# Queries and keys made once for all heads, scores for two heads together, and three smaller edits in a four-stage megakernel

## The reference, cut to what matters

```python
x = x + 0.5 * ffn0(layernorm(x))      # gate and up to 352, silu, down; inputs and weights rounded to FP4 by blocks of 16
x = x + mamba(layernorm(x))           # 2 layers: 256 channels, 16 states, scan over 256 steps, softplus for the step size
x = x + 0.5 * ffn0(layernorm(x))
x = x + 0.5 * moe(layernorm(x))       # 8 experts, 128 -> 512 -> 128; weight p where p > 0.5, p = sigmoid(x @ Wg + bg)
x = x + attention(layernorm(x))       # 16 heads of 8, causal, relative bias; LayerNorm with gain and shift inside
x = x + 0.5 * moe(layernorm(x))
# attention: q = proj(Wq) / sqrt(8); k = proj(Wk); v = proj(Wv)
#            softmax(q @ k.T + bias[distance], causal) @ v, then @ Wo.T
# rounding:  scale = max(|block|) / 6; q = nearest of 0, .5, 1, 1.5, 2, 3, 4, 6 of |x / scale|, times sign and scale
```

## Time and profile before

| | |
|---|---|
| median of 3 runs | 2702.1 us |
| the profiled execution | 2699.89 us |
| its span, first to last instruction | 2698.1 us |
| PE busy | 2506.0 us, 93% |
| DVE busy | 1943.5 us, 72% |
| ACT busy | 1612.1 us, 60% |
| POOL busy | 1367.7 us, 51% |
| mean granted TensorE clock | 0.969 |
| DMA | 56 GB/s on the mean |

### The profile page before, as it was taken

How to read it: one execution, slowest core, us unless ns; L and a number is a source line. 1 busy time by engine, 2 the same in 40 slices (tenths; PEclk the granted TensorE clock), 3 DMA queues, 4 the chain that set the end, 5 groups by cost and what they waited for, 6 DMA issues and landing times.

```text
span 2698.1 us, 41593 instructions
## 1 busy us (share of the span) xinstructions
PE 2506.0 (93%) x14781; PEld 1756.5 (65%) x14781; DVE 1943.5 (72%) x3913; ACT 1612.1 (60%) x3465; POOL 1367.7 (51%) x1227
## 2 busy tenths in 40 slices
PE   7999999997898999887899999998999999999988
PEld 7888885785565655655555765756556656566665
DVE  5878798789787788687787688788787868532420
ACT  1424436443886567653776558664976786466754
POOL 1466474847373656456363745557373738321111
PEclk9999999998998999998999999998999999999989
DMA  4123121312121113112120212122120213000000
GB/s 153 52 75 102 46 90 48 94 56 71 42 85 32 56 47 96 45 58 63 47 80 33 78 41 63 48 67 63 40 87 29 79 41 94 17 5 1 1 5 5
DMA packets 88573, 150.59 MB, mean 56 GB/s; under 512 B 10565, under 2 KB 21485, under 8 KB 88110
## 3 DMA queue, kind: packets, MB, share of 16 engines
q1 hardware_dynamic: 88366, 147.94, 17.8%
HBM read 145.26 MB, written 2.65 MB: 55 GB/s over the span
## 4 chain that ended last, share of the span: by engine, by line
PE 75%; ACT 10%; DVE 8%; issue 4%; POOL 3%; DMA 0%; POOLq 0%; SPq 0%; DVEq 0%; ACTq 0%
PE c_bank L1369 16%; PE c_bank L924 15%; PE c_bank L916 14%; PE a_bank L762 7%; PE a_bank L752 3%; PE b_bank L1083 2%; DVE hst L710 2%; PE b_bank L1072 2%; PE a_bank L731 2%; PE b_bank L584 2%; ACT weighted_y L959 1%; DVE a_bank L704 1%; PE b_bank L565 1%; PE a_bank L768 1%; PE a_bank L736 1%
## 5 line engine op out<-in xcount | busy, mean ns | idle before, releaser
L833 POOL TENSOR_TENSOR prod_c<-hst,prod_c 128x512 f32<-128x512 f32 x512 | 666.3, 1307 | 411.1 <-DVE hst L710 384.0
L710 DVE TENSOR_TENSOR_SCAN hst<-dA,a_bank 128x512 f32<-128x512 f32 x512 | 621.8, 1214 | 14.8 <-ACT dA L822 4.5
L822 ACT ACTIVATE dA<-delta,a_neg 128x510 f32<-128x510 f32 x512 | 364.7, 719 | 320.5 <-DVE hst L710 314.8
L916 PE MATMUL c_bank<-c_xT,w 128*128 128x512 f32 x1024 | 532.4, 624 | 23.5 <-ACT weighted_y L959 11.8
L924 PEld LDWEIGHTS c_bank<-w,hid 128*128 128x128 f32 x4096 | 487.5, 192 | 57.9 <-ACT hid L951 26.8
L1369 PEld LDWEIGHTS c_bank<-ident 128*128 128x128 f32 x4004 | 484.6, 193 | 47.8 <-issue 39.3
L924 PE MATMUL c_bank<-w,hid 128*128 128x128 f32 x4096 | 511.1, 277 | 1.6 <-ACT hid L951 1.5
L1369 PE MATMUL c_bank<-ident 128*128 128x128 f32 x4004 | 491.8, 277 | 0.3 <-ACT weighted_y L959 0.3
L951 ACT ACTIVATE hid<-c_bank,b 128x512 f32<-128x512 f32 x512 | 349.1, 687 | 150.0 <-PE c_bank L916 147.4
L975 POOL TENSOR_TENSOR xs<-xs,weighted_y 128x512 f32<-128x512 f32 x128 | 167.5, 1309 | 497.3 <-ACT weighted_y L959 496.2
L704 DVE TENSOR_TENSOR a_bank<-du,a_bank 128x512 f32<-128x512 f32 x512 | 349.8, 683 | 72.6 <-PE a_bank L752 69.9
(11 more groups left out here) (182 smaller groups left out, 3159.8 us busy)
## 6 DMA issues: line engine op xcount, KB each, us to landing
prod_c<-c_rows SPq DMA_DIRECT2D x512, 256.0 KB, 3.2
w<-in_w SPq DMA_DIRECT2D x2, 2048.0 KB
xs<-in_x SPq DMA_DIRECT2D x8, 256.0 KB, 7.2
bias<-skew SPq DMA_DIRECT2D x1, 2048.0 KB, 8.4
out_dram<-xs SPq DMA_DIRECT2D x8, 256.0 KB, 2.3
in_wT<-in_in_wT SPq DMA_DIRECT2D x1, 512.0 KB
c_rows<-bcC SPq DMA_DIRECT2D x16, 32.0 KB, 1.6
b_hq<-in_w_gu SPq DMA_DIRECT2D x1, 384.0 KB, 3.3
```

What stands on the lines that cost most here:

```text
L710: nc.vector.tensor_tensor_scan(hst[:, s % RS, :], dA[:, s % RA, :], b_bank, 0.0, ALU.mult, ALU.add).then_inc(M.h.sem, 1)
L822: nc.scalar.activation(half_batches(dA[:, s % RA, :], 1), half_batches(delta[:, h, :], 1), ACT.Exp, scale=a_neg[:, l, h, n:n + 1]).then_in ...
L833: nc.gpsimd.tensor_tensor(prod[:, s % RP, :], hst[:, s % RS, :], cring[:, s % RC, :], ALU.mult).then_inc(M.pp.sem, 1)
L916: nc.tensor.matmul(S.bank[up_bank(e, c)][:, :], w1[:, e, c * 128:(c + 1) * 128], S.xT[:, :], start=True, stop=True).then_inc(M.up.sem, 1)
```

## The change

1. **q and k.** The weights are laid out once, with no copies. One k product into bank 1 and one q product into bank 0 for each group. ACT copies q once, DVE clears the lower 12 bits of q and k and subtracts (four operations for each group where there were sixteen). SP writes the two parts to DRAM, six DMAs of 256 KB into `qk_rows`, waits for them, and reads them back in eight DMAs (four strips for q, four for k) in the threefold layout. The first scores wait for these.
2. **Scores.** Two heads at a time, one into bank 0 and one into bank 1. Both transposes of the exponentials go through bank 2, which also holds the products with v; so each fourth transpose waits for DVE's division as well. The exponentials have four buffers, not three.
3. **Quantizer.** The subtraction (L509) moves from DVE to POOL, ahead of the rescaling.
4. **Softplus.** The larger of x and 0 is combined with the correction term while ACT takes the logarithm; behind the logarithm stands one addition instead of two operations.
5. **Gate and division.** The gate's factor 0.5 is folded in (one DVE operation fewer for each mixture pass), and the division by the row sums is one DVE operation, not two.
6. **Order strings.** All five are written anew; 1987 spare products instead of 2002; SP has a lane b.

```diff
 ORDER_PE = (
-    "b2d10bd53bd4b2d7b2d8b2d31bd4b3d43b5dbd61adbda3b2d10b2ad6ab2a2d7ad27ad4bd9b3ad6ad28a2d4ad8ad2ad5ad13a2d9ad14"
+    "b2d9bd48bd4b2d7b2d7b2d33bd4b3d43b5dbd58ad4a3bd4b2d2ad3b2dad3b2a2d5ad27ad6bd9b3ad6ad29a2d10ad14a2d8ad8ad8b5ab"
...
 ORDER_PE = (
...
-    "c2bcbc2bc2bc74")
+    "b2cbc2bcb2cbc2bcb2cb6d4b3d7bd4b3d8bd4bd4bd4bd4b4d28c68")
...
 ORDER_SP = (
-    "a215c2a73caca64caca73ca62ca39c3")
+    "a165b2ab2a65c2a5b2a2b2a59c2a7b2a2b2a55c2a2b2ab2a65cb2ab2a53baba3b2a8ca33b4cb4c2")
...
-        pr = att_buf[:, 768:1920].rearrange("p (b n) -> p b n", b=3)
+        pr = att_buf[:, 768:2304].rearrange("p (b n) -> p b n", b=4)
...
             if rounded is not None:
-                nc.vector.tensor_tensor(xq, xq, c, ALU.subtract).then_inc(rounded.sem, 1)
+                ins.then_inc(rounded.sem, 1)
...
+            nc.gpsimd.tensor_tensor(q[0][:, 0:n], q[0][:, 0:n], q[1][:, 0:n], ALU.subtract).then_inc(L.sem, L.one())
+            yield
+            pool.wait_ge(L.sem, L.n)
             nc.gpsimd.tensor_tensor(dst.rearrange("p (b s) -> p b s", s=BLK), q[0][:, 0:n].rearrange("p (b s) -> p b s", s=BLK),
...
+            for h in range(HALVES):
+                dve.wait_ge(L.sem, step[h])
+                nc.vector.scalar_tensor_tensor(out=delta[:, h, :], in0=S.bank[h][:, :], scalar=0.0, in1=delta[:, h, :],
+                                               op0=ALU.max, op1=ALU.subtract).then_inc(L.sem, L.one())
...
-                nc.vector.tensor_tensor(xc[:, h, :], xc[:, h, :], delta[:, h, :], ALU.subtract).then_inc(L.sem, L.one())
-                yield
-                dve.wait_ge(L.sem, L.n)
-                nc.vector.scalar_tensor_tensor(out=delta[:, h, :], in0=S.bank[h][:, :], scalar=0.0, in1=xc[:, h, :],
-                                               op0=ALU.max, op1=ALU.add).then_inc(M.delta.sem, 1)
+                nc.vector.tensor_tensor(delta[:, h, :], delta[:, h, :], xc[:, h, :], ALU.add).then_inc(M.delta.sem, 1)
...
+            dve.wait_ge(M.qE.sem, L.at(M.qE, 1))
+            nc.vector.tensor_scalar(q_hi.bitcast(I32), q_lo.bitcast(I32), TOP12, None, ALU.bitwise_and).then_inc(M.qH.sem, 1)
+            yield
+            dve.wait_ge(M.k.sem, L.at(M.k, 1))
+            nc.vector.tensor_scalar(k_hi.bitcast(I32), S.bank[1][:, :].bitcast(I32), TOP12, None, ALU.bitwise_and).then_inc(M.kH.sem, 1)
+            yield
+            dve.wait_ge(M.qH.sem, L.at(M.qH, 1))
+            nc.vector.tensor_tensor(q_lo, q_lo, q_hi, ALU.subtract).then_inc(M.qS.sem, 1)
+            yield
+            dve.wait_ge(M.kH.sem, L.at(M.kH, 1))
+            nc.vector.tensor_tensor(k_lo, S.bank[1][:, :], k_hi, ALU.subtract).then_inc(M.kS.sem, 1)
+            yield
...
-            for g in range(HG):
-                if g:
-                    pe.wait_ge(M.qE.sem, L.at(M.qE, g))
-                nc.tensor.matmul(S.bank[0][:, :], wqT[:, g, :], S.xT[:, :], start=True, stop=True).then_inc(M.q.sem, 1)
-                yield
-                if g:
-                    pe.wait_ge(M.kH.sem, L.at(M.kH, g))
-                nc.tensor.matmul(S.bank[1][:, :], wkT[:, g, :], S.xT[:, :], start=True, stop=True).then_inc(M.k.sem, 1)
-                yield
+            nc.tensor.matmul(S.bank[1][:, :], wkT[:, :], S.xT[:, :], start=True, stop=True).then_inc(M.k.sem, 1)
+            yield
+            nc.tensor.matmul(S.bank[0][:, :], wqT[:, :], S.xT[:, :], start=True, stop=True).then_inc(M.q.sem, 1)
+            yield
...
+            def scores(r, queries, keys, part):
+
+                b, h = r // HEADS, r % HEADS
+                p0, s0 = 32 * (h % 4), b * SEQ
+                return nc.tensor.matmul(S.bank[r % 2][:, part], qT[p0:p0 + 3 * DH, h // 4, s0 + queries:s0 + queries + 128],
+                                        kT[p0:p0 + 3 * DH, h // 4, s0:s0 + keys], start=True, stop=True)
...
+                        pe.wait_ge(s_qk, 16 * 8 * (L.g + 1))
+                        pe.wait_ge(M.kS.sem, L.at(M.kS, 1))
...
+                    if w:
+                        pe.wait_ge(M.m.sem, L.at(M.m, 2 * w))
+                    for r in (2 * w, 2 * w + 1):
+                        scores(r, 128, 256, slice(0, 256))
+                    scores(2 * w, 0, 128, slice(256, 384))
+                    scores(2 * w + 1, 0, 128, slice(256, 384)).then_inc(M.s.sem, 1)
+                    yield
...
+        def b_sp(sp, L):
+
+            for g in range(GROUPS):
+                L.g = g
+                rows = a["qk_rows"][g]
+                sp.wait_ge(att.qH.sem, L.at(att.qH, 1))
+                for p in (0, 1):
+                    sp.dma_start(rows[0, p], q_hi).then_inc(s_qkd, 16)
+                sp.wait_ge(att.kH.sem, L.at(att.kH, 1))
+                for p in (0, 2):
+                    sp.dma_start(rows[1, p], k_hi).then_inc(s_qkd, 16)
+                yield
+                sp.wait_ge(att.qS.sem, L.at(att.qS, 1))
+                sp.dma_start(rows[0, 2], q_lo).then_inc(s_qkd, 16)
+                sp.wait_ge(att.kS.sem, L.at(att.kS, 1))
+                sp.dma_start(rows[1, 1], k_lo).then_inc(s_qkd, 16)
+                yield
+                sp.wait_ge(s_qkd, 16 * 6 * (g + 1))
+                for i in range(2):
+                    strips = rows[i].rearrange("p (i j g) n -> (p i) j g n", i=DH, j=4)
+                    dst = qk[:, i, :, :].bitcast(F32)
+                    for j in range(4):
+                        sp.dma_start(dst[32 * j:32 * j + 3 * DH, :, :], strips[:, j, :, :]).then_inc(s_qk, 16)
+                    yield
```

336 lines of the change are left out of this document (142 added, 194 removed).

## The result

The changed kernel takes 2632.2 us (median, 2628.19 to 2634.66) against 2703.1: ratio 0.9736, interval 0.9718 to 0.9755, 2.6% faster. Timed again beside later experiments it took 2633.0 us, ratio 0.9749 (0.9731 to 0.9767), though single runs then went from 2626 to 2642. The forecast was 2618, range 2570 to 2680.

A forecast was written before the change was run, and what follows sets the result against it. The prediction took PE to bound most of the kernel. Its terms, 41.3 + 38.4 + 3.3 + 5 - 5 = 83 us, came off 2699.9 us, giving 2616.9, or 2619 beside the median; it predicted 2618 us, range 2570 to 2680.

The forecast's parts named there:

- The bound: PE, busy 93% of the span and 75% of the chain of waits, bounds most of the program.
- The sign of being wrong that I gave: PE's idle time growing much beyond 192 us while its real work falls by 80: new order or DVE's maxima bound.
- Part 1: q and k products on PE, 32 each down to 8 each: 48 x 0.86 = 41.3 us go.
- Part 2: Scores on PE in pairs of heads, 0.44 us instead of 0.74: 38.4 us gained, bounds nothing and 47.4.
- Part 3: Spare products on PE: 15 fewer, 3.3 us; 28 ahead of the last mixture, 5 us gained (bounds 0 and 6).
- Part 4: q and k through DRAM before each group's first scores: trip about 15 us, bounds 12 and 25; 5 us lost.
- rival D: Slower by SP's queue: 30 us trips give 2710 us; decides from a trip of 28 us on; chance 0.10.
- The covers: PE work ordered behind each group's q product to hide the DRAM trip: 13.0 to 24.2 us, 142 in all.
- Part 5: Other engines: DVE loses 156 us, 17 gained; POOL gets 79 more, 5 lost; the rest set off, counted zero.
- Rival C: POOL's subtraction comes onto the chain, half of 48 delaying lane a: 50 us, 2668 us; chance 0.12.
- The sum: Whole kernel: 41.3 + 38.4 + 3.3 + 5 - 5 = 83 us gained, 2618 us predicted, 3.1% faster.
- Rival B: More comes free: lighter DVE takes a fifth of PE's holes, 40 us, giving 2578 us; chance 0.12.

The follow-up runs named there:

- after: The changed kernel itself, with all parts of the change, against the kernel before: 2632.2 us, ratio 0.9736; timed again 2633.0 us, ratio 0.9749.
- x2: Changed kernel with each group's q and k product made four times over into the same bank: 2674.7 us, ratio 0.9902 to the kernel before.
- x12: Kernel before with 3 of 4 q and k products only 8 columns wide, all else kept: 2696.3 us, ratio 0.998.
- x1: Changed kernel with both heads of a pair read from one 32-partition strip instead of two: 2668.9 us, ratio 0.9879 to the kernel before.
- x7: Changed kernel without the 28 spare products before the last mixture: 2641.8 us, ratio 0.9765 to the kernel before.
- x9: Changed kernel with 18 more spare products before the last mixture pass but one: 2635.0 us, ratio 0.9752 to the kernel before.
- x3: Changed kernel without the q and k transfers through DRAM from the second group on: 2623.1 us, ratio 0.9712 to the kernel before.
- x4: Changed kernel with the quantizer's subtraction back on DVE and GpSimd's piece left empty: 2647.8 us, ratio 0.9803 to the kernel before.
- x11: Kernel before with only the quantizer's subtraction moved from DVE to GpSimd: 2713.8 us, ratio 1.0051.
- x6: Changed kernel with SP's reads of q and k right behind its writes: 2634.9 us, ratio 0.9754 to the kernel before.
- x5: Changed kernel with q and k tile rows 16 bytes apart, so reads go as 2 KB pieces: 2639.3 us, ratio 0.9771 to the kernel before.

## Why the prediction was right, and where it was not

**The bound.** Right for after, wrong in its wording: "work taken from PE shortens the time nearly one for one". x2 shows that work added costs one for one. x12 shows that 32 us taken from the kernel before, with its order and the steps of ACT and DVE between the products as they were, give 5. An order written by hand has no work waiting to fill a hole. That the change got its gain because the order was written anew around the shorter work is argued, not shown: no run has the new strings without the parts, or the parts without the strings. The sign of being wrong that I gave came half true: PE's idle time grew by 19 us while its work fell by 91. It is not DVE's two maxima, for which PE itself does not wait and its weight loads wait 3.8 us; nor has another engine replaced the bound.

**Part 1, q and k.** 41.3 us expected, 43.6 gone from PE (60.6 to 17.0), 45 when put back (x2). 16 and 16 records, as expected.

**Part 2, the pairs, is the term that was mis-sized on PE.** I took 0.44 us for a pair, since no row showed weight loads side by side; it is 0.375, the upper bound. 47.7 us left PE, not 38.4, and x1 gives 32 to 39 of time for one step between. The rule of the Trainium skill that I weighed (TensorE: Matmul & The Clock Gate, Part 3: Packing small matmuls), that matmuls in different row groups run at the same time and a weight load overlaps them, gave the right number here.

**Part 3, the spares.** The 15 fewer are 3.3 us. The last mixture's clock is 0.99 as said; x7 puts the 28 between 2.5 and 9 us, not told from nothing by the interval. What I missed is that the order lost 40 spares one mixture earlier (putting 18 back changed nothing, x9), and that the clock fell behind lane a as a whole, from 0.98 to 0.94.

**Part 4, the way through DRAM.** The step that failed is the landing of the reads. The steps ahead of them came about as counted: the writes landed 7.8 to 8.2 us after the q product's start in five of the groups, and my terms give 7.9. But I gave the last of eight reads the 3.2 us that one transfer of C rows takes, and it took 8.5 to 11.7, with the DMA engines 0.83 busy and not 0.20. Mamba's waits on SP between the writes' landing and the first read, which I did not count either, added 1.7 to 4.9 us in four groups, 4.1 in the first. So the trip took 19.2 to 28.9 us, 23.4 on the mean, where I had 15; it was my upper bound of 25 that came near, and one group passed the 28 from which rival D was to decide. The covers failed the other way: I counted 142 us of PE's work in all, and x3 shows 181 until PE's order comes to the scores, since PE waits for other things in there as well. With the trips and the covers as measured, the trip overruns in four groups, by 5.1, 3.0, 1.0 and 1.3 us. That is 10.4 us, close to the 9.7 that PE waited and the 6.5 to 9 that x3 won back. The way of pricing holds; both of its inputs were too small, and the 5 us taken came out near by luck, because the two errors offset each other.

**Part 5, DVE and GpSimd, counted zero.** GpSimd at 1439 us is near the 1447 expected, DVE at 1821 gave up 123 us and not 156, of which 24.8 were a misreading: the softplus has two operations in these places after as before (46.7 us, now 50.0), and only one of them moved ahead of the logarithm. GpSimd's subtraction at 1557 ns is a little shorter than the 1.64 I had on the mean. In the changed kernel the move is worth 18 us (x4), in the kernel before it costs 14 (x11). A share of 8% of the chain did not price it. That the place in the orders of DVE and GpSimd decides the sign is the likely reason, not shown: x4 and x11 differ also in the q and k part and the scores, and DVE may count for more once PE has less to do. What the softplus, the gate and the division are worth no run tells. Rival C, a later lane a, did not come with the new order: it ends its last layer at 2227 us, 90 earlier.

**The sum.** 83 forecast, 71 measured. Rival B, PE's holes filling by themselves, did not come: they grew by 19 us. The sum had no term for the 18.3 us that the part behind lane a grew by, and counted zero for DVE and GpSimd, where x4 shows 13 to 18 us; it is luck that these two nearly offset each other. Undone one at a time, the parts are worth 39 + 45 + 18 - 6.5 = 95.5 us, 25 more than the whole. Much of that surplus is the clock of the single runs: at one clock it is 32 + 40 + 13 - 7 = 78, 7 more than the whole. By PE's own account, 91 us of work went and 19 of idle time came. The rows of that exchange among PE's waits, before (us in total, times, longest):

```profile
PE a_bank L752 <- DVE hst L710: 42.0, 39, 3.2
...
PE c_bank L916 <- ACT hid L951: 9.0, 7, 2.5
...
PE c_bank L901 <- ACT gwT L943: 2.9, 5, 0.7
```

And after:

```profile
PE a_bank L754 <- DVE hst L712: 21.4, 17, 4.0
...
PE c_bank L915 <- ACT hid L950: 12.9, 15, 2.3
...
PE c_bank L900 <- ACT gwT L942: 11.3, 10, 2.1
...
PE b_bank L1048 <- DMA q_and_k<-qk_rows: 9.7, 3, 5.0
```

The wait on the scan was halved, with a lighter DVE; the mixture's waits on ACT and the new one on DMA took its place. Of the 19 us, 12 stand behind lane a. What would bring them back is not settled. Without the trip 6.5 to 9 us come; spares against the lower clock gave nothing net. No run moves the first of the last four mixture passes back under lane a, which is what the cut of the span points at, and none but x3, which leaves the transfers out, beats the changed kernel.

## What to carry to other kernels

Price work on a busy engine from both sides: what it costs to add need not be what it gives to remove, when a fixed order stands around it (45 us for 41 added, 5 for 32 removed). Count a wait once: PE and its weight loads stand still for the same transfer, and a view that adds them shows 24.0 us where PE idles 9.7 and removing the trip gives 6.5 to 9. A wait that is only pushed along a shared queue comes back in another lane (x6). A trip through DRAM is priced by all its bytes on the DMA engines, not by one transfer's landing. And cut the span where a lane ends: the gain can be made in one part and lost again in the other.

## What the runs showed of the hardware

- Two products of 24 rows in different 32-row strips and different banks, f32, run side by side fully, weight loads of 128 columns included: 0.375 us for two heads, 0.603 in one strip, about 0.37 for one alone.
- A read from DRAM into 24 partitions as 8 KB pieces took 0.60 us for each piece in the records, a write of 2 KB pieces 0.085 us. With the pieces cut to 2 KB (x5) the trips were no shorter.
- The way through DRAM, 1.5 MB out in six transfers and 1.5 MB back in eight, never took less than 18.7 us with the steps around it (x6; 19.2 in after), though one 256 KB write is listed at 2.6 us from issue to landing. The DMA engines were 0.83 busy while the reads were under way.
- At the lower clock a 512-column f32 record takes 853 ns from start to start, at the higher 430. Between two runs of the same kernel, 31 us more at the lower level went with 14.1 us more of busy PE and 13.5 of time.
- Spares kept the clock up where PE had waited 6.3 us (1.00 in x9), and it fell after the next gaps.
